# Window attention on one core: the weighed sum with the values as the standing operand, on four column groups

## What is computed

```python
h = _ln(x, ln1_g, ln1_b)
h = jnp.roll(h, (-s, -s), axis=(1, 2))
win = _window_partition(h, w)
qkv = win @ qkv_w + qkv_b
...
attn = jnp.einsum('bnhd,bmhd->bhnm', q, k) * hd ** (-0.5)
attn = attn + bias.transpose(2, 0, 1)[None]
...
attn = jax.nn.softmax(attn.reshape(nB, nh, N, N), axis=-1)
out = jnp.einsum('bhnm,bmhd->bnhd', attn, v).reshape(nB, N, C)
out = out @ proj_w + proj_b
...
x = x + out
h2 = _ln(x, ln2_g, ln2_b)
h2 = jax.nn.gelu(h2 @ fc1_w + fc1_b) @ fc2_w + fc2_b
return x + h2
```

## Time and profile before

| | us |
|---|---|
| median of 3 runs | 516.42 |
| lowest, highest | 514.03, 518.35 |
| span of the profiled execution, first to last instruction | 516.1 |
| one group of 8 steps, mean of five in mid-kernel | 39.36 |

### The profile page before, as it was taken

How to read it: one execution, slowest core, us unless ns; L and a number is a source line. 1 busy time by engine, 2 the same in 40 slices (tenths; PEclk the granted TensorE clock), 3 DMA queues, 4 the chain that set the end, 5 groups by cost and what they waited for, 6 DMA issues and landing times.

```text
span 516.1 us, 21507 instructions
## 1 busy us (share of the span) xinstructions
PE 462.7 (90%) x9630; PEld 352.7 (68%) x9630; DVE 388.9 (75%) x549; ACT 359.0 (70%) x501; POOL 384.4 (74%) x376
## 2 busy tenths in 40 slices
PE   0765799999899999999999999998799999999995
PEld 0533587787788788778788778677566666666664
DVE  2865688899779899879899899894467767666752
ACT  0236488878878878778778778775577777777761
POOL 2648959879969979969969978942288888888830
PEclk9998799999999999999999999999999999999999
DMA  8201424411411411411011011000003303311333
GB/s 162 60 1 31 99 47 96 114 34 25 104 38 30 104 39 28 102 34 37 23 29 40 23 25 41 24 23 3 3 3 84 84 12 74 84 46 40 83 83 83
DMA packets 9986, 27.04 MB, mean 52 GB/s; under 512 B 3368, under 2 KB 3368, under 8 KB 7976
## 3 DMA queue, kind: packets, MB, share of 16 engines
q1 hardware_dynamic: 9896, 25.68, 21.1%
HBM read 9.15 MB, written 8.39 MB: 34 GB/s over the span
## 4 chain that ended last, share of the span: by engine, by line
PE 53%; DVE 17%; POOL 16%; ACT 8%; issue 2%; DMA 2%; SPq 0%; ACTq 0%; DVEq 0%
PE work L693 20%; PE outs L693 10%; POOL probs L367 9%; PE trans L693 8%; PE scores L693 6%; DVE negmax L482 5%; DVE probs L476 4%; POOL stat_rstd L333 4%; PE scores L829 3%; PE trans L789 3%; DVE x L517 3%; DMA params<-in_params 2%; POOL xn L344 2%; DVE x L533 2%; ACT qT L605 2%
## 5 line engine op out<-in xcount | busy, mean ns | idle before, releaser
L367 POOL TENSOR_TENSOR probs<-probs,negmax 128x1024 f32<-128x1024 f32 x64 | 123.9, 1937 | 38.4 <-DVE negmax L482 38.4
L333 POOL TENSOR_TENSOR stat_rstd<-stat_var,minus_half 128x8 f32<-128x8 f32 (+1 forms) x62 | 105.0, 1693 | 5.0
L476 DVE TENSOR_TENSOR probs<-scores,bias 128x1024 f32<-128x1024 f32 x64 | 77.9, 1218 | 32.9 <-PE scores L693 32.9
L638 ACT ACTIVATE probs<-probs 128x1024 f32<-128x1024 f32 x64 | 67.7, 1058 | 50.3 <-POOL probs L367 49.8
L338 POOL TENSOR_TENSOR xn<-x,stat_mean 128x256 f32<-128x256 f32 (+1 forms) x91 | 77.2, 867 | 4.1
L482 DVE TENSOR_REDUCE negmax<-probs 128x16 f32<-128x1024 f32 x64 | 78.1, 1220 | 2.2
L693 PEld LDWEIGHTS work<-params,probs 128*64 128x64 f32 x2048 | 62.2, 138 | 23.5 <-DVE x L570 20.5
L693 PE MATMUL scores<-kX,qT 32*64 32x128 f32 x2048 | 71.5, 276 | 7.2 <-DVE probs L476 4.6
L693 PE MATMUL outs<-vX,probsT 128*64 128x34 f32 x2048 | 72.9, 226 | 5.1 <-ACT probsT L643 4.1
L693 PEld LDWEIGHTS outs<-vX,probsT 128*64 128x64 f32 x2048 | 66.0, 139 | 16.4 <-issue 9.5
L789 PEld LDWEIGHTS trans<-ident,probs 128*128 128x128 f32 x512 | 56.2, 142 | 26.4 <-issue 14.2
(11 more groups left out here) (64 smaller groups left out, 691.7 us busy)
## 6 DMA issues: line engine op xcount, KB each, us to landing
kX<-kT SPq DMA_DIRECT2D x124, 64.0 KB, 2.0
x<-in_x SPq DMA_DIRECT2D x32, 224.0 KB
out<-x SPq DMA_DIRECT2D x28, 224.0 KB
x<-in_x SPq DMA_DIRECT2D x32, 32.0 KB
out<-x SPq DMA_DIRECT2D x28, 32.0 KB
out<-x SPq DMA_DIRECT2D x16, 56.0 KB
params<-in_params SPq DMA_DIRECT2D x1, 741.5 KB, 12.3
out<-x SPq DMA_DIRECT2D x16, 8.0 KB
```

The costliest lines, as they stand in the source:

```text
L333: nc.gpsimd.tensor_tensor(stat_rstd[:, cols], stat_var[:, cols], minus_half[:, cols], ALU.pow).then_inc(ln_rstd, pieces)
L367: nc.gpsimd.tensor_tensor(e, e, top, ALU.add).then_inc(shifted, 1)
L476: nc.vector.tensor_tensor(e[:, :].rearrange("q (u a m) -> q a u m", u=2, a=2), scores[:, :].rearrange("q (a u m) -> q a u m", a=2, u=2), b ...
L638: nc.scalar.activation(probs[n % 4][:, :], probs[n % 4][:, :], ACT.Exp)\
```

## The change

In the weighed sum the operands change places. The values stand (128 rows x 32 columns: two heads of one window, zero where the column's head is not the row's), the probabilities move (64 columns), and the output has channels on the partitions, so it needs no transposes. 16 such matmuls a step lie on four column groups of 32. The sums of the probabilities come from 4 more matmuls a step, with a standing block of ones (`head_ones`) and 256 moving columns each; they give every sum 16 times, once for each channel of its head, beside the outputs' own layout. `divide` therefore takes 256 reciprocals a row and multiplies 256 by 256 elements, straight into `oT`. `transpose_o`, its copy on ScalarE (`copy_oT`) and `o_rows` go. The outputs use both PSUM banks in turn.

The values come out of the projection with one copy of 128 x 512 on ScalarE into `v_rows`, in the place of two copies of 64 x 512, and four DMAs an image place them in `vX`. There, two neighbouring columns of a standing operand lie 64 bytes apart. The order of windows and heads in the scores, the bias and the projection's weights changes with it, at equal sizes.

```diff
-VW = 2 * (HD + 1)
+VW = 2 * HD
...
-        vX = [sb(f"vX{i}", 32, VW) for i in range(2)]
+        v_rows = [sb(f"v_rows{i}", VW, 8, 2) for i in range(2)]
+        vX = [sb(f"vX{i}", 2, VW, 8, 2) for i in range(2)]
+        head_ones = sb("head_ones", VW)
...
-        inverse = [sb(f"inverse{i}", 16) for i in range(2)]
+        inverse = [sb(f"inverse{i}", 2 * P) for i in range(2)]
...
+            def spread_values(of, i):
+
+                par = i % 2
+                sp.wait_ge(v_copied, COUNT["V", of, i])
+                for p in range(2):
+                    for odd in range(2):
+                        sp.dma_start(vX[par][N * odd:N * (odd + 1), p, HD * odd:HD * (odd + 1)],
+                                     v_rows[par][N * p:N * (p + 1), HD * odd:HD * (odd + 1)])\
+                          .then_inc(vX_loaded[par], 16)
...
             def divide(n):
 
-                o = outs[:, 0:16 * (HD + 1)].rearrange("q (t d) -> q t d", d=HD + 1)
+                g, step = divmod(n, STEPS)
+                bank = outs[n % 2]
                 dve.wait_ge(outs_ready, n + 1)
-                nc.vector.reciprocal(inverse[n % 2][:, :], o[:, :, HD]).then_inc(inverse_ready, 1)
+                nc.vector.reciprocal(inverse[n % 2][:, :], bank[:, 2 * P:4 * P]).then_inc(inverse_ready, 1)
                 dve.wait_ge(inverse_ready, n + 1)
-                nc.vector.tensor_tensor(o_rows[n % 2][:, :].rearrange("q (t d) -> q t d", d=HD),
-                                        o[:, :, 0:HD],
-                                        inverse[n % 2][:, :].unsqueeze(2).to_broadcast([P, 16, HD]),
-                                        ALU.mult).then_inc(outs_taken, 1)
+                dst = oT[g % 2][:, :].rearrange("q (a i r) -> q i a r", i=2 * STEPS, r=WIN)
+                nc.vector.tensor_tensor(
+                    dst[:, 2 * step:2 * step + 2],
+                    bank[:, 0:2 * P].rearrange("q (i a r) -> q i a r", i=2, r=WIN),
+                    inverse[n % 2][:, :].rearrange("q (i a r) -> q i a r", i=2, r=WIN),
+                    ALU.mult).then_inc(outs_taken, 1)
...
                 elif kind == "V":
-                    for p in range(2):
-                        half = slice(N * p, N * (p + 1))
-                        src = work2[half, :].rearrange("q (w a) -> q w a", w=2)[:, :, 0:4 * C]
-                        dst = vX[par][half, :, (HD + 1) * p:(HD + 1) * p + HD]
-                        done = nc.scalar.activation(
-                            dst.rearrange("q (w a) d -> q w a d", w=2),
-                            src.rearrange("q w (a d) -> q w a d", d=HD), ACT.Copy)
-                    done.then_inc(v_copied, 1)
+                    image = GI * of + i
+                    if image >= 2:
+                        act.wait_ge(vX_loaded[par], 16 * VX_DMAS * (image // 2))
+                    src = work2[:, :].rearrange("q (a z) -> q a z", a=8)[:, :, 0:C]
+                    nc.scalar.activation(v_rows[par][:, :, :, :],
+                                         src.rearrange("q a (e b) -> q e a b", b=2), ACT.Copy)\
+                      .then_inc(v_copied, 1)
...
             def weigh(n):
                 image, k = divmod(n, 2)
+                bank = outs[n % 2]
                 if k == 0:
-                    copied("V", image // GI, image % GI)
+                    pe.wait_ge(vX_loaded[image % 2], 16 * VX_DMAS * (image // 2 + 1))
                 pe.wait_ge(trans_copied, n + 1)
-                if n:
-                    pe.wait_ge(outs_taken, n)
+                if n >= 2:
+                    pe.wait_ge(outs_taken, n - 1)
...
+                tiles = [(slice(32 * (2 * p + a), 32 * (2 * p + a + 1)), p, a) for p in range(2) for a in range(2)]
                 for u in range(2):
-                    for h in range(HEADS):
-                        for w in range(2):
-                            at = (u * HEADS + h) * P + w * N
-                            row = (w * 4 + 2 * k + u) * HEADS + h
-                            out = outs[w * N:(w + 1) * N, u * HEADS * VW:(u + 1) * HEADS * VW]\
-                                .rearrange("q (p h d) -> q p h d", p=2, h=HEADS)[:, :, h]
-                            done = mm(out, probsT[n % 2][:, at:at + N], vX[image % 2][:, row, :])
+                    for w in range(2):
+                        for rows, p, a in tiles:
+                            at = (4 * u + 2 * a + p) * P + w * N
+                            mm(bank[rows, u * P + w * N:][:, 0:N],
+                               vX[image % 2][:, p, :, 4 * w + 2 * k + u, a],
+                               probsT[n % 2][:, at:at + N])
+                for rows, p, a in tiles:
+                    both = probsT[n % 2][:, :].rearrange("q (u t m) -> q t u m", u=2, m=P)
+                    done = mm(bank[rows, 2 * P:4 * P].rearrange("q (u m) -> q u m", u=2),
+                              head_ones[:, :], both[:, 2 * a + p])
                 done.then_inc(outs_ready, 1)
```

More of the change, by code:

```diff
@@ L215, in build @@
         kX_loaded = [sem(f"kX_loaded{i}") for i in range(2)]
+        vX_loaded = [sem(f"vX_loaded{i}") for i in range(2)]
         ln_sum, ln_mean, ln_centred = sem("ln_sum"), sem("ln_mean"), sem("ln_centred")
@@ L244, in build @@
         KX_DMAS = 4
+        VX_DMAS = 4
         def means_before(G, i):
@@ L289, in _ @@
                         spread_keys(of, i)
+                    elif kind == "V":
+                        spread_values(of, i)
                 if n in (1, STEPS - 2):
@@ L422, in _ @@
             for t in range(2):
-                done = nc.vector.memset(vX[t][:, :, :], 0.0)
-            done.then_inc(vX_zeroed, 1)
+                nc.vector.memset(vX[t][:, :, :, :, :], 0.0)
+            nc.vector.memset(head_ones[:, :], 0.0).then_inc(vX_zeroed, 1)
             dve.wait_ge(vX_zeroed, 1)
[L426 to L429, removed]
+            for odd in range(2):
+                done = nc.vector.memset(head_ones[N * odd:N * (odd + 1), HD * odd:HD * (odd + 1)], 1.0)
             done.then_inc(zeroed, 1)
@@ L445, in _ @@
             dve.wait_ge(params_in, 16)
-            for t in range(3):
-                last = nc.vector.tensor_scalar(wqkv[:, t, :], wraw[:, t, :], gain[:, 0:1], None,
-                                               ALU.mult)
+            nc.vector.tensor_scalar(wqkv[:, 0:2, :], wraw[:, 0:2, :], gain[:, 0:1], None, ALU.mult)
+            for k in range(2):
+                of = slice(C * k, C * (k + 1))
+                last = nc.vector.tensor_scalar(
+                    wqkv[:, 2, of].rearrange("q (o d a) -> q a o d", o=2, a=2),
+                    wraw[:, 2, of].rearrange("q (a o d) -> q a o d", a=2, o=2), gain[:, 0:1], None,
+                    ALU.mult)
             last.then_inc(params_ready, 1)
@@ L452, in _ @@
             dve.wait_ge(y_bias_summed, 1)
-            nc.vector.tensor_tensor(y_bias[:, :], outs[:, 0:C], bproj[:, :], ALU.add)\
+            nc.vector.tensor_tensor(y_bias[:, :], outs[0][:, 0:C], bproj[:, :], ALU.add)\
               .then_inc(y_bias_made, 1)
@@ L458, in _ @@
                     continue
[L460 to L463, removed]
+                m = mask[:, j * P:(j + 1) * P].rearrange("q (p m) -> q p m", p=2).unsqueeze(2)\
+                    .to_broadcast([P, 2, 2, N])
                 for at in ((0, 1), (2,))[j]:
-                    nc.vector.tensor_tensor(
-                        bias[:, at, :].rearrange("q (h p m) -> q h p m", h=HEADS, p=2), r, m,
-                        ALU.add).then_inc(bias_made, 1)
+                    for a in range(2):
+                        r = rpb[:, a * P:(a + 1) * P].rearrange("q (o m) -> q o m", o=2).unsqueeze(1)\
+                            .to_broadcast([P, 2, 2, N])
+                        done = nc.vector.tensor_tensor(
+                            bias[:, at, a * 2 * P:(a + 1) * 2 * P].rearrange("q (p o m) -> q p o m", p=2, o=2),
+                            r, m, ALU.add)
+                    done.then_inc(bias_made, 1)
             dve.wait_ge(bias_made, 3)
@@ L778, in score @@
                                 rows = slice(32 * (2 * w + hh), 32 * (2 * w + hh + 1))
[L779 to L780 removed]
+                                to = hh * BANK + (2 * u + p) * P
+                                out = scores[w * N:(w + 1) * N, to:to + P].rearrange("q (o m) -> q o m", o=2)
                                 done = mm(out, qT[two][rows, at:at + N], kX[two][rows, :, at:at + N])
@@ L810, in weigh @@
-                done.then_inc(outs_ready, 1)
-            def transpose_o(n):
-                pe.wait_ge(outs_taken, n + 1)
-                if n:
-                    pe.wait_ge(oT_copied, n)
-                for u in range(2):
-                    done = nc.tensor.transpose(outsT[:, u * P:(u + 1) * P],
-                                               o_rows[n % 2][:, u * P:(u + 1) * P], ident[:, :])
-                done.then_inc(oT_ready, 1)
+                    for w in range(2):
[4 more added lines that the diff above has]
```

(1 more changed line is left out.)

27 lines of the change are left out of this document (6 added, 21 removed).

## The result

The changed kernel takes 570.17 us (median of 4 runs, 569.28 to 571.20) and the kernel before, beside it, 516.51: a ratio of 1.105, 95% interval 1.101 to 1.108. The forecast was 560 in a range of 542 to 612.

The account below looks back on a forecast made before the run. TensorE was taken as nearest the bound before, VectorE as the bound after, through longer reciprocals. Groups growing 5.6 us, counted 7.5 times, give 42, plus 2 of tail: 516.4 + 44 = 560 us, range 542 to 612.

Parts of the forecast that it names:

- the reciprocal's slope: VectorE's divide: 5.6 ns an element, so 256 reciprocals take 1.58 us, 1.33 us more a step.
- VectorE's gaps: VectorE in a group of 8 steps: 0.5 us for exposed waits on top of 45.0 us busy.
- the bias of the projection: VectorE's output-projection bias (L517), held while GpSimd works: gets shorter, giving back 0.5 us a group.
- The count of groups and the tail: Attention's eight groups count as 7.5, giving 42 us; the last three divisions in the tail add 2 us.
- Rival 2: VectorE's reciprocal has a steeper slope, 8.3 ns an element, 2.25 us for 256: 602 us, up to 660; chance 0.14.
- rival 3: TensorE's four column groups don't run side by side: 3.2 us more a step, 697 us; chance 0.04 with no overlap.
- The strided loads: TensorE's weight loads, columns 64 bytes apart: no cost at double time per column, 0.6 us a step at four times.
- the bias addition that I named: Sign in the profile after: TensorE waits for VectorE's bias addition, while VectorE's wait for scores is gone.
- the first step: Kernel before, attention: TensorE busy 37.6 of 39.36 us a group, nearest to the bound; VectorE has 5.0 us left.
- rival 1: VectorE's reciprocal excess is a fixed part, 0.50 us for 256 elements: 511 us, from 505 to 520; chance 0.20.
- their own deadline: Values' DMAs: wanted 12 us after their copy, against 6.6 us for queue and landing, so cost 0.
- If the cover went: Values' DMAs in SyncE's queue, no longer hidden: 1 to 2 us an image, 30 to 60 in all.

Follow-up runs that it names:

- run 2: Kernel before, with one more reciprocal of 256 elements a row each step, its result unused: 582.99 us, ratio 1.128.
- run 3: Kernel before, with one more reciprocal of 64 elements a row each step, its result unused: 522.70 us, ratio 1.011.
- run 6: Changed kernel with a copy for the reciprocal, and weights read from 32 adjacent columns (other values weighed): 517.62 us, ratio 1.0023.
- run 1: Changed kernel with a plain copy in place of the reciprocal, so outputs are multiplied by the sums: 519.38 us, ratio 1.0058.
- run 7: Changed kernel with a copy for the reciprocal and without the matmuls of ones (the copy reads the outputs): 516.86 us, ratio 0.9999.
- run 8: Changed kernel with neither copy nor reciprocal, outputs multiplied by a tile of ones, sums still computed: 520.35 us, ratio 1.0083.
- run 9: Kernel before, with the first LayerNorm's power of groups 1 to 7 moved from GpSimd to ScalarE: 509.61 us, ratio 0.9871.
- run 10: Changed kernel with a copy for the reciprocal and the first LayerNorm's power of groups 1 to 7 on ScalarE: 518.22 us, ratio 1.0024.
- run 12: As run 10, but without the values' DMAs; waits on them become waits on the copy, values' weights stay zero: 511.44 us, ratio 0.9917.

## Why the prediction was right, and where it was not

**VectorE: right in kind, short in size.** The term that was mis-sized is the reciprocal's slope: 5.6 ns an element was forecast, from a fixed part of 158 taken from other instructions, and 6.25 with a fixed part of 147 is what runs 2 and 3 show. 1.75 us for 1.58, +1.50 a step for +1.33, 1.3 us a group, the whole of 46.3 against 45.0 and of the 10 us between 560 and 570. That the excess belongs in the slope and not in the fixed part was a choice with one size to go by; the forecast said so, and it came out well. The other terms of a group held: VectorE's gaps, 46.28 - 45.73 = 0.55 for 0.5; the bias of the projection at 1626 ns for 1847, two a group, 0.44 for 0.5; ScalarE gives up 4.8 us a group for 5. The count of groups and the tail held in their sum only: 42 + 2 us were forecast for groups that grow by 5.6, which at the measured 6.92 is 52 + 2, and the traces have 50.3 and 3.6. Rival 2's eight steps an element would be 8.3 ns. The Trainium skill ("VectorE: DVE Perf Modes", Walkthrough, First, the fixed hardware budget) gives the reciprocal a repeat count of 8; the runs show 6.25/1.04 = 6.0 of the engine's steps, so, read as eight steps an element, as the forecast read it, the count gives too high a price. By the row's slope the forecast was nearer.

**TensorE: right.** 1.13 us for the weighed sum, its parts 0.57 and 0.56 for 0.62 and 0.51, against 4.5 that rival 3 had for no overlap and 2.3 for two at a time: four groups of 32 columns at 128 rows do run side by side, and rival 3 is out. The strided loads, which the forecast could not price, cost 0.10 us of that. The Trainium skill ("SBUF — State Buffer", Specifications) has a penalty for each crossing to a new line of 16 bytes, and run 6 agrees that there is one: 153 ns against 111. That is a factor of 1.4, where the forecast had looked at two and four.

**The waits: right for VectorE, in part for TensorE.** VectorE waits for nothing. TensorE waits for VectorE, but the bias addition that I named is 7.3 us of it, the sums that add the projected output 23.6, and a further 18.1 is for ScalarE's copy of the queries.

**What bounds the kernel: wrong, without harm.** "So TensorE is nearest to the bound (96%)" was the first step, and rival 1's 511 us was built on it, with the cheapest reciprocal giving back TensorE's 1.2 us a group. Runs 1, 7 and 8 show that neither a shorter TensorE nor a shorter VectorE by itself moves the changed kernel far from 39.8 us a group (39.4 and 40.2), and run 9 that the kernel before gains 1.3% when GpSimd gives up an addition and a power a piece, 49 us from 75 to 352 us, while TensorE's busy time is as before. The Trainium skill ("Trainium Kernel Development and Optimization", Performance Expectations, Reading a trace) calls matmul busy time a bad metric for how close a kernel is to its roofline, because matmuls are pipelined. Run 7, 19 us less busy and no faster, fits the warning; its reason no run here tests. GpSimd's 33.5 of 39.4 us is a mean, and hid that in some of the steps it was full.

**The DMAs: right only as far as VectorE covered them.** The forecast compared the values' own landing with their own deadline, 12 us against 6.6, and no wait for `vX` ever showed, in any run. The cost went to the neighbours in the queue instead, the keys and a load of images: runs 10 and 12 put it at 1.1% or 6 us. "If the cover went, 1 to 2 us an image, 30 to 60 in all" was far too much, and the sign named, a wait for `vX`, was the wrong tile.

**What stays open**: the last half per cent between runs 9 and 12, the share of the DMAs in run 1's missing gain, and which engines together set the period once the divide is cheap.

## What to carry to other kernels

Count the elements of a reciprocal before moving a normalisation: dividing by a sum that is already spread over the columns costs VectorE 6.25 ns for each, six times an addition or a product, and here 16 sums a row became 256 elements, each sum sixteen times over. Ask of an added DMA not only when its own data are wanted but what stands behind it in its queue. And before naming an engine as the bound by a mean over a group, look whether another is full in single steps; taking one piece of work away from it tells more than any share.

## What the runs showed of the hardware

- The reciprocal of f32 is a straight line over 16, 64 and 256 elements a row: 147 ns and 6.25 ns an element. Right behind another reciprocal the one of 16 takes 194 ns for 247 (runs 2 and 3).
- Four matmuls on groups of 32 columns with 128 rows run side by side: 32 records of 64 columns hold TensorE for 0.57 us, 8 of 256 for 0.56. On two groups of 64, 32 records of 34 columns held it for 1.05.
- Weight loads of 32 columns take 153 ns with the columns 64 bytes apart and 111 with adjacent ones; 0.10 us in 32 of them reach TensorE's order of time.
- A power on GpSimd takes 1.65 us for 8 elements a row; logarithm and exponential of the same 8 on ScalarE take 302 and 209 ns:

```profile
L333 POOL TENSOR_TENSOR stat_rstd<-stat_var,minus_half 128x8 f32<-128x8 f32 x60 | 98.9, 1648 | 4.7
```

```profile
L644 ACT ACTIVATE stat_var<-stat_sq,eps 128x8 f32<-128x8 f32 x28 | 8.5, 302 | 0.3
L647 ACT ACTIVATE stat_rstd<-stat_var 128x8 f32<-128x8 f32 x28 | 5.8, 209 | 0.9
```

- In three of the five groups of the changed kernel TensorE's granted clock is 0.96 in the mean (two of them are shown above). In the first of them that is one stretch at 0.50, the level of 1.2 GHz, from 129.4 to 132.6 us; ahead of it TensorE had waited 2.32 us for VectorE. With VectorE the bound it cost nothing that shows: these groups are as long as the others. In run 10 a stretch at 0.50 about as long came in a group 3.3 us longer than run 12's.
